# A ranking network on one core: which engine fetches and places the embedding rows of two fields, and in what batches

## What is computed

```python
x0 = emb[ids].reshape(ids.shape[0], -1)
x = x0
for i in range(3):
    s = x @ cross_w[i]
    x = x0 * s[:, None] + cross_b[i] + x
h = relu(x0 @ w1 + b1)      # 1664 -> 1024
h = relu(h @ w2 + b2)       # 1024 -> 512
h = relu(h @ w3 + b3)       # 512 -> 256
return sigmoid(concatenate([x, h], axis=1) @ out_w + out_b)
```

## Time and profile before

| | before |
|---|---|
| median of 3 runs | 515.7 us (515.51 to 515.76) |
| the profiled execution's own time | 515.57 us |
| its span (first to last instruction) | 513.8 us |
| TensorE busy | 478.8 us, 93% of the span |
| VectorE busy | 247.9 us, 48% |
| ScalarE busy | 33.5 us, 7% |
| GpSimd busy | 372.1 us, 72% |
| mean granted clock of TensorE | 0.992 of full speed |

### The profile page before, as it was taken

How to read it: one execution, slowest core, us unless ns; L and a number is a source line. 1 busy time by engine, 2 the same in 40 slices (tenths; PEclk the granted TensorE clock), 3 DMA queues, 4 the chain that set the end, 5 groups by cost and what they waited for, 6 DMA issues and landing times.

```text
span 513.8 us, 13128 instructions
## 1 busy us (share of the span) xinstructions
PE 478.8 (93%) x2912; PEld 444.7 (87%) x2912; DVE 247.9 (48%) x490; ACT 33.5 (7%) x68; POOL 372.1 (72%) x400
## 2 busy tenths in 40 slices
PE   2699899998998999899899999999999899999997
PEld 1399798898998889899799989888898889999996
DVE  5776446354363635436264443645454263544335
ACT  4642000000000000000000000000000000000112
POOL 5777777777777777777777777777777777777740
PEclk9999999999999999999899999999999899999999
DMA  7981111111111111111111111111111111111100
GB/s 223 385 300 29 29 28 26 31 27 27 29 29 28 26 32 27 28 30 27 28 28 30 28 28 30 29 26 28 29 28 26 31 28 26 28 29 26 27 18 2
DMA packets 18142, 24.61 MB, mean 48 GB/s; under 512 B 7845, under 2 KB 8832, under 8 KB 18064
## 3 DMA queue, kind: packets, MB, share of 16 engines
q0 software_dynamic: 12576, 12.90, 11.3%
q1 hardware_dynamic: 4154, 9.71, 5.3%
q10 hardware_dynamic: 1334, 1.17, 0.7%
HBM read 24.41 MB, written 0.01 MB: 48 GB/s over the span
## 4 chain that ended last, share of the span: by engine, by line
PE 61%; POOL 18%; issue 11%; DMA 6%; DVE 3%; ACT 0%; POOLq 0%; DVEq 0%
PE l_bank L733 50%; POOL x_raw L345 18%; DMA x_raw<-in_L_rec_emb,idx 6%; PE x_bank L745 4%; PE x_bank L733 2%; PE h_bank L787 2%; DVE x_raw L510 2%; PE l_bank L818 1%; PE h_bank L757 1%; DMA ids<-in_r_ids 1%; PE h_bank L829 0%; PE l_bank L757 0%; DVE xT_lo L534 0%; PE h_bank L733 0%; DVE xT_hi L517 0%
## 5 line engine op out<-in xcount | busy, mean ns | idle before, releaser
L345 POOL DMA_INDIRECT x_raw<-in_L_rec_emb,idx x393 | 371.2, 945 | 122.2 <-issue 107.6
L733 PE MATMUL l_bank<-w_hi,xT_hi 128*128 128x342 f32 (+1 forms) x624 | 144.9, 333 | 0.1
L733 PE MATMUL l_bank<-w_lo,xT_hi 128*128 128x342 f32 (+1 forms) x624 | 138.5, 322 | 0.0
L733 PE MATMUL l_bank<-w_hi,xT_lo 128*128 128x342 f32 (+1 forms) x624 | 138.1, 321 | 0.0
L733 PEld LDWEIGHTS l_bank<-w_lo,xT_hi 128*128 128x128 f32 x624 | 107.3, 191 | 0.0
L733 PEld LDWEIGHTS l_bank<-w_hi,xT_hi 128*128 128x128 f32 x624 | 105.0, 192 | 2.6 <-DVE xT_lo L534 0.4
L733 PEld LDWEIGHTS l_bank<-w_hi,xT_lo 128*128 128x128 f32 x624 | 106.9, 191 | 0.0
L517 DVE CAST xT_hi<-x_bank 128x512 fp32r<-128x512 f32 (+2 forms) x56 | 33.1, 592 | 94.2 <-PE x_bank L745 94.2
L510 DVE COPY_PREDICATED x_raw<-past,x_bank 128x512 f32<-128x512 int32 (+1 forms) x66 | 40.3, 610 | 57.4 <-DMA x_raw<-in_L_rec_emb,idx 56.9
L745 PE MATMUL x_bank<-identity,x_raw 128*128 128x128 f32 x208 | 34.8, 280 | 17.0 <-DVE x_raw L510 16.9
L733 PE MATMUL l_bank<-w_hi,h1T_hi 128*128 128x512 f32 x120 | 48.7, 406 | 0.9 <-DVE h1T_lo L539 0.9
(11 more groups left out here) (97 smaller groups left out, 310.4 us busy)
## 6 DMA issues: line engine op xcount, KB each, us to landing
ids<-in_L_rec_emb SPq DMA_DIRECT2D x1664, 0.2 KB
ids<-in_L_rec_emb ACTq DMA_DIRECT2D x1280, 0.2 KB
w_raw<-in_L_rec_w SPq DMA_DIRECT2D x18, 512.0 KB, 14.6
x_raw<-in_L_rec_emb,idx POOLq DMA_INDIRECT x393, 2.4
b_rows<-in_L_rec_b ACTq DMA_DIRECT2D x1, 512.0 KB
b_rows<-in_L_rec_b ACTq DMA_DIRECT2D x1, 256.0 KB
ids<-in_r_ids SPq DMA_DIRECT2D x1, 208.0 KB, 2.6
b_rows<-in_L_rec_b ACTq DMA_DIRECT2D x1, 128.0 KB
```

The lines of the kernel that those rows point to most:

```text
L345: pool.indirect_dma_start(out=dst, out_offset=None, in_=emb, in_offset=rows).then_inc(landed, 16)
L733: done = pe.matmul(bank[:, 0:b - a], x[:, k, :], w[:, k, a:b], start=(k == 0 and n == 0), stop=(k == last_k and n == 2))
```

## The change

ScalarE no longer places rows, makes no `h1_hi(0)`, and in the last tile leaves the first two `x_hi` copies and `h2_hi(14)` to VectorE. It fetches field 20 for 13 tiles (2 to 6, 8 to 15), three more than before: tiles 2, 12 and 15. GpSimd gathers 390 fields where it gathered 393. ScalarE's fetching begins just ahead of `x_hi(0, 3)` with 16 rows, goes on with 16, and then in batches of 32 rows without any other work between, until all 1664 rows are issued; then come the copies of the last tile from group 2 on. The only waits that are left in it are those for a free side buffer. VectorE places both fields in `place(t, g)`, at the start of `make_whole` of the group that holds them.

```diff
-    ACT_TILES = [3, 4, 5, 6, 8, 9, 10, 11, 13, 14]
+    ACT_TILES = [2, 3, 4, 5, 6, 8, 9, 10, 11, 12, 13, 14, 15]
     ACT_FIELD = GROUPS[2][-1] * FPK
     ACT_BUFS = 2
-    ACT_SHARES = [24, 28, 24, 28]
+    ACT_FIRST = 16
+    ACT_REGS = 32
...
                     if g == 1:
                         load_rows()
+                    if g == NG - 1:
+                        act.wait_ge(sp_idx_ready, 1)
+                        fetch(ACT_FIRST)
                     x_hi(0, g)
-                h1_hi(0)
-
-            def step(t):
-                if t in SP_TILES or t in ACT_TILES:
-                    act.wait_ge(x_transposed, NG * t + 1)
-                if t in SP_TILES:
-                    sp_place(t)
-                if t in ACT_TILES:
-                    act_place(t)
-                for share in ACT_SHARES:
-                    fetch(share)
+                fetch(ACT_REGS - ACT_FIRST)
+                while fetched[0] < P * len(ACT_TILES):
+                    fetch(ACT_REGS)

             def last_step(t):
-                assert t not in SP_TILES and t not in ACT_TILES
-                x_hi(t, 0)
-                h2_hi(t - 1)
-                for g in range(1, len(LAST_GROUPS)):
+                for g in range(2, len(LAST_GROUPS)):
                     x_hi(t, g)
...
+            def place(t, g):
+                if t in SP_TILES and SP_FIELD // FPK in groups(t)[g]:
+                    i = SP_TILES.index(t)
+                    dve.wait_ge(sp_landed[i % SP_BUFS], 16 * P * (i // SP_BUFS + 1))
+                    dve.tensor_copy(x_buf[t % 2][:, SP_FIELD * E:(SP_FIELD + 1) * E], sp_rows[i % SP_BUFS]).then_inc(sp_placed, 1)
+                if t in ACT_TILES and ACT_FIELD // FPK in groups(t)[g]:
+                    j = ACT_TILES.index(t)
+                    dve.wait_ge(act_landed[j % ACT_BUFS], 16 * P * (j // ACT_BUFS + 1))
+                    dve.tensor_copy(x_buf[t % 2][:, ACT_FIELD * E:(ACT_FIELD + 1) * E], act_rows[j % ACT_BUFS]).then_inc(act_placed, 1)
+
             def make_whole(t, g):
+                place(t, g)
...
             def h1_lo(t):
                 for half in range(2):
-                    if t > 0:
-                        h1_hi(t, half)
+                    h1_hi(t, half)
...
             def last_step(t):
                 make_whole(t, 0)
+                x_hi(t, 0)
                 x_lo(t, 0)
                 l2_out(t - 1)
+                h2_hi(t - 1)
                 h2_lo(t - 1)
                 make_whole(t, 1)
+                x_hi(t, 1)
                 x_lo(t, 1)
```

More of the change, by code:

```diff
@@ L50, in dcn_ranker_kernel @@
     SP_BUFS = 4
-    ACT_TILES = [3, 4, 5, 6, 8, 9, 10, 11, 13, 14]
+    ACT_TILES = [2, 3, 4, 5, 6, 8, 9, 10, 11, 12, 13, 14, 15]
     ACT_FIELD = GROUPS[2][-1] * FPK
     ACT_BUFS = 2
-    ACT_SHARES = [24, 28, 24, 28]
-    assert all(sum(ACT_SHARES) * (t - 1) >= P * (j + 1) for j, t in enumerate(ACT_TILES))
-    ONE_RUNS = [(SP_FIELD, range(2, TILES - 1)), (ACT_FIELD, range(3, 7)), (ACT_FIELD, range(8, 12)), (ACT_FIELD, range(13, 15))]
+    ACT_FIRST = 16
+    ACT_REGS = 32
+    ONE_RUNS = [(SP_FIELD, range(2, TILES - 1)), (ACT_FIELD, range(2, 7)), (ACT_FIELD, range(8, 16))]
     AT_ROWS = [(f, t) for f, tiles in ONE_RUNS for t in tiles]
@@ L370, in load_rows @@
                     act.dma_start(rows[:, :], vec.rearrange("(o n) -> o n", o=1).broadcast_to([P, rows.shape[1]])).then_inc(rows_loaded, 16)
[L372 to L376, removed]
             fetched = [0]
@@ L394, in fetch @@
                     share -= rows
[L396 to L400, removed]
             def x_hi(t, g):
@@ L406, in x_hi @@
                                x_bank[g % 2][:, 0:len(ks) * P], ACT.Copy).then_inc(xT_hi_ready, 1)
[L408 to L417, removed]
             def h2_hi_last(t):
@@ L468, in _ @@
             first_step()
-            act.wait_ge(sp_idx_ready, 1)
-            for t in range(1, TILES - 1):
-                step(t)
             last_step(TILES - 1)
```

## The result

The changed kernel takes 536.66 us (median of 4 runs, 535.59 to 537.19) against 515.7: a ratio of 1.0405, 95% interval 1.0386 to 1.0423. The prediction was 539.6 us in a range of 530 to 548. The profiled execution took 535.59 us with a span of 533.8; the median lies 1.1 us above it.

The account below looks back on a forecast made before the run. ScalarE's row issue was taken to bound the changed kernel: last row at 514.6 us, so the last tile's copy comes 24.0 us later; 515.57 + 24.0 = 539.6 us, other terms counted at 0, range 530 to 548.

Parts of the forecast that it names:

- The bound moves to ScalarE's issue: GpSimd's gathers set the pace before; ScalarE's nearly full issue queue takes over, 9.0 to 9.25 us a batch, chance 0.68.
- The price of a batch: ScalarE's 32 rows: load 2.18, 0.2 around it, 31 spacings of 0.216, 9.1 us (9.09); last row at 514.6.
- rival 4: ScalarE's batches dearer: rows at 0.221 and loads of 2.3, 9.35 us a batch, time about 553; chance 0.07 for over 548.
- The last tile: ScalarE's copy `x_hi(15, 2)` stands behind its last row DMA: 514.6 instead of 490.59, 24.0 us later, the chain after it unchanged.
- The late tiles: ScalarE's rows late for `make_whole`: tile 6 about 8 us, again from tile 12, tile 14 19 us; not added to its issue.
- tile 7 "gives back" the wait: Tile 7 has no field for ScalarE to fetch, so it gives back tile 6's lateness of about 8 us.
- What was counted at nothing: VectorE's 26 placements (0 to 0.3 us each) and moved copies (some 0.6 each), SyncE's later buffers, covered first rows: 0.
- The clock: TensorE's last-tile wait of 3.9 us, or 2.4, might lower its clock; 1.5 us left to the range.
- The faster one: ScalarE at SyncE's 8.22 us a batch, GpSimd still the bound: 3.7 us won, 511.9; chance 0.06 faster, 0.02 no change.
- The second: ScalarE and SyncE slow each other's issuing; ScalarE speeds up after SyncE ends, 7.4 us less, 532.2; chance 0.12.
- The two batches of SyncE: SyncE's 32 rows took 5.99 us beside ScalarE's issuing and 5.96 without, so no issuer slows the other.
- VectorE's copies and GpSimd: VectorE's plain copies might shut GpSimd out: 26 of 0.22, up to 5.7 us, 515 to 518, if ScalarE reached SyncE's pace.

Follow-up runs that it names:

- e1: Changed kernel with ScalarE's old ten fields (tiles 3 to 6, 8 to 11, 13, 14), all else kept: 515.68 us, ratio 1.0000 to the kernel before.
- e3: Changed kernel with register loads of 16 in place of 32, still 13 fields: 559.1 us, ratio 1.0843 to the kernel before.
- e4: Changed kernel with all `x_hi` copies of the last tile on VectorE, none behind ScalarE's last row: 533.09 us, ratio 1.0340 to the kernel before.
- e5: Changed kernel with eleven fields on ScalarE (tiles 2 to 6, 8 to 11, 13, 14): 521.94 us against 516.49 for the kernel before, ratio 1.0108.
- e6: Changed kernel with SyncE fetching only tiles 2 to 5 and GpSimd gathering the nine fields: 534.89 us against 516.49 for the kernel before, ratio 1.0357.

## Why the prediction was right, point by point

*The bound moves to ScalarE's issue.* Right and shown: two thirds of the chain are `ACTq`, e1 removes 21 us by taking three fields away, e3 adds 22 us by adding loads alone.

*The price of a batch.* Forecast 9.09, measured 9.0. The load was right (2.18 against 2.20); the spacing of rows was 0.212 where 0.216 was read from a few batches. The last row was out at 510.6 and not at 514.6. That is the term that was mis-sized, by 4.0 us in 514.6, and it makes the difference in the span (537.8 forecast, 533.8 measured). The time is off by 2.9 only, since the median of the changed kernel lies 1.1 us above its profiled execution; that part is luck. And one price for every row was itself too simple: what a row costs depends on its id, as the last section shows. The run of 28.45 us from which rival 4 took its dearer rows has 17 rows inside the table, the run of 27.90 us has 13.

*The last tile.* Right: the copy follows the last row within 0.05 us, and from it to the end are 23.16 us, as in the kernel before (513.8 - 490.59 = 23.2). e4 shows what it is worth by itself: little, because field 20 of tile 15 is just as late.

*The late tiles.* Tile 6 was late by 8 (224.88 against 216.77) as forecast. Tile 14's repair was forecast at about 479 and ran at 474.86, earlier by the same error of the batch. Placements waited for rows in tiles 5, 6, 12, 13 and 14, as forecast; in tile 12 it was 0.6 us, with a longer wait for gathers behind it. One sentence misleads: that tile 7 "gives back" the wait. It does for ScalarE's queue, not for the time. In the changed kernel that doesn't show, because the queue sets the end whatever happens before; in e5, where the queue ends early, 5.7 of 7.9 us stay.

*What was counted at nothing.* The placements by VectorE (0.18 to 0.2 us in 21 of 26, where 0 to 0.3 was allowed, but up to 0.43), the copies moved in tile 0 and the last tile, the 16 rows ahead of `x_hi(0, 3)`, SyncE's later buffers: together at nothing, by e1. The reason given for the copies of the last tile reads the rows loosely: ScalarE's copy of group 2 waited 5.40 us for TensorE, so what they could use up was that wait.

*The clock.* TensorE's wait in the last tile was forecast at 2.4 to 3.9 us and was 2.86. The granted clock behind it stayed at 1.00, the upper of the two levels (2.4 GHz), so leaving the 1.5 us out was right. Around tile 6's wait of 8.97 us it was mostly (0.60) and then wholly (0.50) at the lower level (1.2 GHz), already during the wait and behind it. The view of windows, with the granted clock third from the end:

```profile
219.00:223.00 4.00, 0.00 (x0) 0.00 (x0) 0.00 (x0) 0.00 (x0) 2.98 (x4) 0.60 0.14 25
223.00:230.00 7.00, 4.25 (x16) 4.28 (x17) 2.65 (x5) 0.00 (x0) 2.83 (x3) 0.50 0.08 17
511.00:515.00 4.00, 3.16 (x22) 3.17 (x22) 1.47 (x5) 0.31 (x2) 0.00 (x0) 1.00 0.00 0
```

*The rivals.* The faster one needed 8.6 us a batch and the mean was 9.0, and what it promised for GpSimd is real but small: with twelve fields, two gathers fewer give 1.2 us. The second, that the two issuers slow each other, fell with e6. The two batches of SyncE that the prediction set against it couldn't decide it, since they differ in their rows: the 5.99 us beside ScalarE's issuing are for 2 rows inside the table, the 5.96 without it for 4. Nine batches of SyncE with 2 such rows took 5.78 us in the mean. The conclusion drawn from them was right by luck. Like set against like, each of SyncE's last four batches takes the same in e1, where ScalarE is silent from 421.6 on, as in the changed kernel, to 0.01 us. The rule of the Trainium skill that the rival leaned on (Perfetto Trace Analysis, DMA Instruction — HWDGE), a lock that one issuer waits for while the other uses the shared block, has no price in time here: the same rows stand 0.212 us apart with SyncE silent and with SyncE issuing.

*VectorE's copies and GpSimd.* The rule of the Trainium skill on VectorE's plain copies (SBUF — State Buffer, Who interferes with whom) says that the one of the two that issues first holds the shared ports and the other is blocked. That GpSimd is held up doesn't show: with 23 such copies e1 takes the time of the kernel before, and GpSimd's gathers stay 1.24 to 1.25 us apart where they run beside copies. The other side does show. A gather and a copy of tile 3 in the changed kernel:

```profile
123.29 0.94 POOL L345 DMA_INDIRECT x_raw<-in_L_rec_emb,idx  x1 [0.30 <-issue]
123.88 0.37 DVE L467 COPY x_raw<-ids 128x64 f32<-128x64 f32 x1
```

The gather ends at 124.23, the copy at 124.25. In the changed kernel five copies began 0.53 to 0.70 us into a gather; they took 0.26 to 0.43 us and all ended 0.02 to 0.05 behind its end. Copies that began within its first 0.5 us took 0.18 to 0.2. So it is VectorE that waits, for the last part of a gather and at most 0.25 us.

## What to carry to other kernels

An engine that issues many small DMAs has a queue to be budgeted like an engine's work, and the busy share doesn't show it: take start-to-start times of the issues and of the register loads from the timeline, multiply, and set the sum against each deadline and against whatever stands behind it in the same queue. Near a full queue the return is a cliff: twelve well placed fields were 1.2 us faster, thirteen 21 us slower. A queue that ends on time must still meet its deadlines in the middle: with eleven fields of which one was 8 us late the kernel was 5.45 us slower (e5). And take the price of an issue from the data that the kernel will see, for here it depends on the ids.

## What the runs showed of the hardware that was not expected

- A register load costs nearly by the register: 1.22 us for 16, 2.20 for 32. That is 0.06 us a register and some 0.25 fixed; with what stands around it and the longer row spacing, a further load cost 0.43 us in e3. So larger loads save little: the 32-row batches brought the price of a row from 0.286 to 0.281 us.
- The price of a row depends on its id. ScalarE's issues last either 0.09 to 0.12 us or 0.23 to 0.55, with nothing between, and it is the same rows that last long in every run. They are the rows whose id lies inside the table, which the ids drawn in the reference's inputs show: 214 of the changed kernel's 1664 are, and these 214 are the long ones. (SyncE: 189 of 1664, 0.23 to 0.32 us against 0.06 to 0.11.) For an id past the table's end the kernel adds the table's length to the row number and issues the DMA with `bounds_check="skip_entire_dma"`. Nothing moves for it: of the 384 rows more than before 44 are inside, and the queue `q10` has 88 packets more, two for each of them (the view of DMA, before and after). In e6 the queue `q1` has 268 packets fewer, and of the 1152 rows that SyncE no longer fetches 134 are inside:

```profile
q10 hardware_dynamic: 1334, 1.17, 0.7%
q10 hardware_dynamic: 1422, 1.18, 0.7%
```

- So although each row is issued as a DMA of 256 bytes, about seven in eight fetch nothing here, and VectorE's repair fills their place. In the changed kernel the row behind a skipped one follows after 0.181 us mostly, the row behind one that moves after 0.33 mostly and 0.39 in the mean; the 23 rows at 0.181 are all skipped ones. A batch of 32 without a single row inside the table took 7.84 us from start to start in the changed kernel, two with nine took 9.57 and 9.96. The rows alone of the first and of one of the two:

```profile
387.68 5.70 ACTq L385 DMA_DIRECT2D ids<-in_L_rec_emb  x32
404.64 7.26 ACTq L385 DMA_DIRECT2D ids<-in_L_rec_emb  x32
```

- If all ids lay inside the table, a batch would cost some 2.4 + 31 x 0.39 = 14.5 us. That is an estimate from the load with what stands around it and these spacings; no run shows it. Most moving rows take 0.24 us and some over 0.4, 52 of 214 in the changed kernel and 90 in e3; why stays open.
- A wait of 2.86 us of TensorE left the granted clock at its upper level, while after one of 2.54 it was 0.57 over 4 us. The length of the last wait alone doesn't tell.
